# A transformer block with self- and cross-attention: GpSimd's part of the first stage moved and reordered, differences issued ahead of bases, and the first cross step's maxima ahead of the next query projection

## The reference

```python
def _attn(xq, ctx, wq, wkv, wo, bo):
    q = _heads(xq @ wq)
    k, v = jnp.split(ctx @ wkv, 2, axis=-1)
    q = _rope(q, sq, cq); k = _rope(k, sk, ck)
    a = jax.nn.softmax(jnp.einsum('bhnd,bhmd->bhnm', q, k) * DH ** (-0.5), axis=-1)
    return jnp.einsum('bhnm,bhmd->bhnd', a, v) ... @ wo + bo
def _adaln(x, c, lw, lb, gw, gb, bw, bb):
    return _ln(x, lw, lb) * (1.0 + (c @ gw + gb)) + (c @ bw + bb)
x = _attn(_adaln(x, ...), _adaln(x, ...), ...) + x
x = _attn(_adaln(x, ...), _ln(context, ...), ...) + x
x = gelu(_adaln(x, ...) @ ff_w1 + ff_b1) @ ff_w2 + ff_b2 + x
```

## Time and profile before

| what | value |
| --- | --- |
| median of 3 runs | 2149.64 us (2148.78 to 2154.3) |
| profiled execution, its own time | 2151.02 us |
| its span | 2149.2 us |
| TensorE busy | 2040.5 us, 95% |
| VectorE busy | 1751.1 us, 81% |
| ScalarE busy | 1429.1 us, 66% |
| GpSimd busy | 18.1 us, 1% |
| mean granted TensorE clock | 0.981 of full speed |

### The profile page before, as it was taken

How to read it: one execution, slowest core, us unless ns; L and a number is a source line. 1 busy time by engine, 2 the same in 40 slices (tenths; PEclk the granted TensorE clock), 3 DMA queues, 4 the chain that set the end, 5 groups by cost and what they waited for, 6 DMA issues and landing times. The chain is left out here.

```text
span 2149.2 us, 43063 instructions
## 1 busy us (share of the span) xinstructions
PE 2040.5 (95%) x17544; PEld 934.3 (43%) x17544; DVE 1751.1 (81%) x2720; ACT 1429.1 (66%) x1844; POOL 18.1 (1%) x16
## 2 busy tenths in 40 slices
PE   4799999999999999999999999999988999979999
PEld 2233333345333334533333453333633455446676
DVE  6899899986999998699989779987588888754754
ACT  4588778774787777577787657786457666652452
POOL 3000000000000000000000000000000000000000
PEclk8899999999999999999999999999998999999999
DMA  6010111011111111111011012021332344333111
GB/s 204 30 40 31 60 40 41 31 60 41 61 41 40 51 41 41 41 60 60 31 41 41 31 51 80 31 56 35 102 113 91 106 145 141 105 101 109 40 40 40
DMA packets 100347, 136.62 MB, mean 64 GB/s; under 512 B 34533, under 2 KB 73399, under 8 KB 100151
## 3 DMA queue, kind: packets, MB, share of 16 engines
q1 hardware_dynamic: 100151, 133.88, 18.9%
HBM read 68.34 MB, written 13.11 MB: 38 GB/s over the span
## 5 line engine op out<-in xcount | busy, mean ns | idle before, releaser
L713 ACT ACTIVATE sa_probs<-sa_ps_s 128x1024 f32<-128x1024 f32 x512 | 496.1, 1022 | 130.9 <-PE sa_ps_s L490 130.8
L505 PE MATMUL sa_ps_o<-sa_probs,sa_v_pair 128*64 128x512 f32 x2048 | 531.0, 609 | 1.4 <-DVE sa_mx L895 1.4
L908 DVE TENSOR_TENSOR sa_acc<-sa_acc,sa_probs 128x1024 f32<-128x1024 f32 x384 | 452.7, 1220 | 19.8 <-ACT sa_probs L713 11.9
L895 DVE CUSTOM_DVE_ANT_0 sa_rise<-sa_ps_t,sa_rise 128x512 f32<-128x512 f32 x504 | 327.3, 687 | 121.8 <-PE sa_ps_t L467 121.6
L483 PE MATMUL sa_ps_s<-scores_or_weights 64*128 64x512 f16 x3072 | 374.8, 376 | 1.5 <-ACT raw_or_keys L687 1.5
L701 ACT ACTIVATE sa_rise<-sa_ps_t 128x1024 f32<-128x1024 f32 x252 | 257.4, 1021 | 140.8 <-PE sa_ps_t L460 139.4
L483 PEld LDWEIGHTS sa_ps_s<-scores_or_weights 64*128 64x128 f16 x3072 | 151.9, 94 | 156.1 <-ACT sa_v_pair L692 6.8
L505 PEld LDWEIGHTS sa_ps_o<-sa_probs,sa_v_pair 128*64 128x64 f32 x2048 | 115.8, 135 | 149.8 <-issue 126.8
L460 PE MATMUL sa_ps_t<-sa_kd,scores_or_weights 64*128 64x512 f16 x504 | 99.3, 389 | 19.3 <-ACT scores_or_weights L697 6.8
L460 PEld LDWEIGHTS sa_ps_t<-sa_kd,scores_or_weights 64*128 64x128 f16 x504 | 25.2, 93 | 201.1 <-issue 163.1
L467 PE MATMUL sa_ps_t<-scores_or_weights 64*128 64x512 f16 x504 | 98.1, 385 | 11.3 <-ACT sa_rise L701 11.2
(11 more groups left out here) (338 smaller groups left out, 3656.2 us busy)
## 6 DMA issues: line engine op xcount, KB each, us to landing
sa_swp<-raw_or_keys SPq DMA_DIRECT2D x124, 256.0 KB, 2.4
sa_inv<-sa_scratch SPq DMA_DIRECT2D x128, 128.0 KB, 2.9
ca_swp<-raw_or_keys SPq DMA_DIRECT2D x64, 256.0 KB, 2.4
ca_inv<-ca_scratch SPq DMA_DIRECT2D x64, 256.0 KB, 3.9
sa_xs<-in_x SPq DMA_DIRECT2D x4, 1024.0 KB, 5.7
sa_xr<-in_x SPq DMA_DIRECT2D x4, 1024.0 KB, 6.8
x_after_cross<-scores_or_weights SPq DMA_DIRECT2D x32, 128.0 KB, 2.2
ff_xr<-x_after_cross SPq DMA_DIRECT2D x4, 1024.0 KB, 6.3
```

The lines of the kernel that those rows point to most:

```text
L505: ins = pe.matmul(ps_o[rows(x), half(c)], v_pair[:, kt, rows(x)], probs[:, kt % 2, c, half(x)], start=(kt == 0), stop=(kt == NK - 1))
L713: act.activation(probs[:, kt % 2, c, :], ps_s[c][:, :], ACT.Exp, scale=float(DH) ** -0.5).then_inc(s_p, 1)
L895: dve.tensor_tensor_reduce(out=larger, in0=max_banks(j, t)[:, half(x)], in1=larger, scale=1.0, scalar=-3.0e38, op0=ALU.add, op1=ALU.max, a ...
L908: dve.tensor_tensor(acc[:, c, :], before, probs[:, kt % 2, c, :], ALU.add).then_inc(s_acc[c], 1)
```

## The change

In self-attention four things are moved. GpSimd now also casts the two halves of the key weights (ScalarE did), as its first work. Its two subtractions for key and query of pair 0 go behind its work on the context, and it waits for the first bases before that. VectorE's weights_low of the key weights stand between the first affines. TensorE issues differences(0, t + 1) ahead of bases(0, t).

In cross-attention bases(0) goes ahead of the projection of query 2 on TensorE, all context values come ahead of both, the gate matmuls go behind project(3), and on VectorE maxima(0) goes ahead of turned(1), while tables() goes to the beginning of step 1. No instruction is added or removed; two casts change their engine.

```diff
--- before.py
+++ after.py
@@ -418,13 +418,14 @@
 
         @block.gpsimd
         def _(pool):
+            for n in range(2):
+                pool.wait_ge(s_w[n // 2], 32)
+                pool.tensor_scalar(weights[n][1], staged[:, n, :], WS, None, ALU.mult).then_inc(s_whi, 1)
             for n in range(4):
                 pool.wait_ge(s_nhi, n + 1)
                 pool.tensor_tensor(norm_out(xT_lo, 0, n), xn_first[:, n, :], norm_out(xT_hi, 0, n),
                                    ALU.subtract).then_inc(s_nlo, 1)
-            for i in range(2):
-                pool.wait_ge(s_hi[i], 1)
-                pool.tensor_tensor(lo[:, 0, i, :], raw[:, i, :], hi[:, 0, i, :], ALU.subtract).then_inc(s_lo[i], 1)
+            pool.wait_ge(s_base, 1)
             pool.wait_ge(s_cst, 7)
             for b in range(B):
                 ins = pool.tensor_scalar(cs[:, b, :], cs[:, b, :], c_mv[:, b, 0:1], c_rstd[:, b:b + 1],
@@ -433,6 +434,9 @@
             for i, op in enumerate((ALU.mult, ALU.add)):
                 pool.wait_ge(s_cn, i + 1)
                 pool.tensor_tensor(cs[:], cs[:], crow[:, i:i + 1, :].broadcast_to([M, B, DC]), op).then_inc(s_cn, 1)
+            for i in range(2):
+                pool.wait_ge(s_hi[i], 1)
+                pool.tensor_tensor(lo[:, 0, i, :], raw[:, i, :], hi[:, 0, i, :], ALU.subtract).then_inc(s_lo[i], 1)
 
         @block.tensor
         def _(pe):
@@ -571,10 +575,10 @@
             pe.wait_ge(s_kq_r[1], 2)
             differences(0, 1)
             for t in range(TT):
-                bases(0, t)
                 if 1 <= t < TT - 1:
                     maxima_free(0, t - 1, 2)
                     differences(0, t + 1)
+                bases(0, t)
                 if t == TT - 2:
                     pe.wait_ge(s_kq_r[0], 4)
                     context_transposes()
@@ -777,7 +781,8 @@
                 normalise(0, q)
             for n in range(4):
                 norm_high(0, n)
-            for n in range(4):
+            act.wait_ge(s_whi, 2)
+            for n in range(2, 4):
                 weights_high(n)
             for i in range(2):
                 for c in range(2):
@@ -1048,7 +1053,9 @@
             tables()
             for n in range(4):
                 first_affine(n)
-            for n in range(4):
+                if n < 2:
+                    weights_low(n)
+            for n in range(2, 4):
                 weights_low(n)
             context_variances()
             dve.wait_ge(s_rope, 32)
@@ -1433,6 +1440,15 @@
                                        xs[:, 4 * (n % 2) + q, n // 2 * P:(n // 2 + 1) * P], ident[:, :])
                 ins.then_inc(s_ntr, 1)
 
+            def gate_products():
+                pe.wait_ge(s_par, 16 * 8)
+                for i in range(2):
+                    for m in range(KD):
+                        for k in range(KD):
+                            ins = pe.matmul(ps_gate[:, i, m, :], gates[:, i, k, m * P:(m + 1) * P], condT[:, k, :],
+                                            start=(k == 0), stop=(k == KD - 1))
+                ins.then_inc(s_gate, 1)
+
             def ff_transposes(n):
                 pe.wait_ge(s_nxc, 2 * TT)
                 for q in range(4):
@@ -1507,31 +1523,29 @@
 
             for pair in range(PAIRS):
                 context_keys(pair)
-            for j in range(3):
+            for j in range(2):
                 for c in range(2):
                     if j >= 1:
                         pe.wait_ge(s_q_r, 2 * (j - 1) + c + 1)
                     project(j, c)
-                if j == 1:
-                    for n in range(2 * B):
-                        context_values(n)
+            for n in range(2 * B):
+                context_values(n)
             pe.wait_ge(s_init, 6)
             pe.wait_ge(s_bo, 32)
             pe.wait_ge(s_cev, 4 * PAIRS // 2)
-            pe.wait_ge(s_par, 16 * 8)
-            for i in range(2):
-                for m in range(KD):
-                    for k in range(KD):
-                        ins = pe.matmul(ps_gate[:, i, m, :], gates[:, i, k, m * P:(m + 1) * P], condT[:, k, :],
-                                        start=(k == 0), stop=(k == KD - 1))
-            ins.then_inc(s_gate, 1)
+            pe.wait_ge(s_low, 1)
+            pe.wait_ge(s_hi, 1)
+            bases(0)
+            for c in range(2):
+                pe.wait_ge(s_q_r, 2 + c + 1)
+                project(2, c)
             pe.wait_ge(s_low, 2)
             for g in range(G):
                 pe.wait_ge(s_hi, g + 1)
                 if g >= 1:
                     pe.wait_ge(s_p, 2 * g)
-                bases(g)
                 if g >= 1:
+                    bases(g)
                     values(g - 1)
                 pe.wait_ge(s_max, g + 1)
                 pe.wait_ge(s_q_r, 2 * min(g + 3, G))
@@ -1567,6 +1581,8 @@
                     if g >= 1:
                         pe.wait_ge(s_sum_r, g)
                     project(g + 3, 1)
+                if g == 0:
+                    gate_products()
                 if g in FF_TRANSPOSE:
                     pe.wait_ge(s_mt_r, g + 1)
                     ff_transposes(2 * FF_TRANSPOSE.index(g))
@@ -1899,10 +1915,14 @@
             low_keys(0)
             turned(0)
             low_keys(1)
+            maxima(0)
             turned(1)
             low(0)
             for g in range(G):
-                maxima(g)
+                if g == 1:
+                    tables()
+                if g >= 1:
+                    maxima(g)
                 if g + 1 < G:
                     low(g + 1)
                 if g >= 3:
@@ -1917,8 +1937,6 @@
                     turned(g + 2)
                 if g in STATS:
                     variances(g)
-                if g == 0:
-                    tables()
                 if g in FF_STATS:
                     ff_variances(g)
                 for u, tiles in enumerate((STATS, FF_STATS)):
```

## The result

The changed kernel takes 2158.24 us (median of 8 runs, 2155.08 to 2161.08) against 2150.26 us (8 runs of before beside them, 2147.28 to 2154.3). The ratio is 1.0034 with an interval of 1.0021 to 1.0047: slower by 0.34%. That is 8.0 us between the medians and 7.3 us (4.5 to 10.1) by the ratio, where 9.0 was forecast. The profiled span is 2154.7 us against 2149.2.

The account below looks back on a forecast made before the run. TensorE, busy 95% of the span, was taken as the bound. Start 1.65, stall and order of differences together 5.75 and cross-attention 1.6 summed to 9.0 us, so 2158.6 us against a median of 2149.64; range 4.4 to 15 us slower.

Parts of the forecast that it names:

- The bound and where to look: TensorE, busy 95%, paces the kernel; delays in the first 75 us of self-attention and 20 us of cross-attention delay everything.
- The stall: Self-attention, pair 0: ScalarE's copy waits for GpSimd's key subtraction behind 7.75 us of context work; relu 2 comes 5.4 later.
- rival (c): Self-attention: not slower, as GpSimd finishes before ScalarE's copy needs it; sum +1.6 us, chance 0.07.
- The round: Maxima loop of pair 0: maxima, differences and bases in series take 2.36 us a round instead of 2.16.
- The start, GpSimd scaling the key weights: Start of self-attention: GpSimd's scalings hold VectorE's small instructions, so TensorE starts at 25.85 instead of 24.21, +1.65 us.
- D: Duration of one GpSimd scaling of a 128x1024 key-weight tile at the start: taken as 2.06 us, bounds 1.0 and 5.3.
- Rival (a): Start: GpSimd is quick at a one-input operation, D 1.0 to 1.5; sum 6.9 to 8.0 us, chance 0.22.
- rival (b): Start: scaling costs per element like the 192-element row, D 3 to 5.3; sum 11 to 15.5 us, chance 0.12.
- Cross-attention: First 20 us of cross-attention: TensorE waits for query 2's copy, gates delay bases(1) by 2.3, 0.81 returns later; +1.6 us.
- Rival (d): Cross-attention gains as its waits of 2.78 and 1.54 us close: -2.4 there, sum 5.0 us, chance 0.15.
- The sum: Whole kernel: 9.0 us slower, a median of 2158.6 us.
- line delay: Cross-attention: the DMA of the line of maxima lies behind a 2 x 256 KB transfer; 0.4 us added, from 0 to 1.3.

Follow-up runs that it names:

- late-subtractions kernel: Kernel before with only GpSimd's two subtractions moved behind the context work, which waits for the first bases: 2157.13 us, ratio 1.0032.
- subtractions-first kernel: Changed kernel, but GpSimd, after waiting for the first bases, makes its two subtractions ahead of the context work: 2150.21 us, ratio 1.0002 to before.
- casts alone: Kernel before with only the two key-weight casts on GpSimd and their weights_low between the affines: 2151.90 us, ratio 1.0003.
- quiet kernel: Kernel before with GpSimd's subtractions after VectorE's last rotation and some weight casts, low parts and context roots moved into ScalarE and VectorE gaps: 2147.53 us, ratio 0.9994.
- early parameters: Kernel before with the eight parameter DMAs of cross-attention's gates issued ahead of the first query's swap: 2149.45 us, ratio 0.9993.

## Why the prediction was right

**The bound and where to look.** Right. TensorE is busy for 95% before and after, no busy time grew on it, and a delay of 7.3 us at the end of pair 0's maxima, with what cross-attention added, came out as 8.0 us of time.

**The stall.** Right in its mechanism and, step by step, in its sizes. With the 0.97 of the start added to each forecast: relu 0 at 44.01 (forecast 44.01), GpSimd let go at 45.70 (45.70), the copy at 55.72 (55.52), relu 2 at 56.22 (56.07), maxima(2) at 57.94 (57.77). Part of this closeness is luck. From the first projection to relu 0 it took 20.75 us in the profile of before and 18.83 in that of the change, the 1.92 forecast; but four other kernels with the subtractions in their old place took 19.69 to 20.23, and the two others with them behind the first bases took 18.00 and 18.05. The first projections' matmuls, in pairs, got faster (from 0.67 to 0.40 us a pair) at 29.7 us in the profile of before and at 30.7 in that of the change, but between 27.0 and 28.4 in these six.

The late-subtractions kernel shows that this part alone is enough, the subtractions-first kernel that without it nothing is left. So rival (c), not slower, falls at the place that the prediction named: the decision was whether GpSimd's 9.8 us of work fits in front of the copy.

**The round.** Mis-sized by 0.09: 2.45 instead of 2.36. Bases to maxima takes 0.68 where I took 0.64, and from the start of maxima to the next differences it is 1.37 where I had 1.32 (and twice 0.61 and 0.08 make 1.30). Over the rounds behind the stall and the last one, that makes maxima(7) 0.4 later, and 0.17 stood already at maxima(2), so stall and order are 7.29 − 0.97 = 6.3 instead of 5.75. The order alone costs 1.9 us in a row of eight rounds without a stall. Behind the stall it costs 0.75: from relu 0 to maxima(7) it is 25.47 us with both (69.48 − 44.01) and 24.72 in the late-subtractions kernel.

**The start, GpSimd scaling the key weights.** This is the term that was wrong in its working: +1.65 forecast, +0.97 in the profile of the change and +0.3 in that of the casts alone. Its steps failed in opposite directions and nearly cancelled. D is 2.77, not 2.06; with it the forecast's own chain would have given over +3. But the step that follows, that tables() is held until the second scaling ends and the first affine starts at 17.7, is false: it started at 15.15. The rows fit a hold of VectorE's instructions with two SBUF tensors for the first 0.9 to 1.0 us of each cast only (below). What followed took longer instead, 10.03 us from the first affine to TensorE's start (25.18 − 15.15) and not 8.15: the first weights_low had to wait for the first cast, which ended at 16.4, and the two of them took 2.05 and 2.17 us beside GpSimd where the chain had 1.15 each. The DMA, too, let GpSimd begin at 13.63 and not at 13.1. Rival (a), a quick cast, and rival (b), one that costs per element like the 192-element row, both lose their condition by D = 2.77, between (a)'s 1.5 and (b)'s 3. The time could not have told this, 8.0 us is also the upper end of (a)'s sum; the rows do.

**Cross-attention.** +1.6 forecast. The mechanism was right: TensorE waits for the copy of query 2 (4.75 us), and the gates (1.95 us) stand in front of bases(1). Counted from the end of ScalarE's copies of values, the copy of query 2 ended 2.0 later than before, where 1.85 was forecast. At bases(1) the kernel with this part alone shows +1.5, where +2.3 was forecast; at step 3 it shows +0.6 to +1.3, by which kernel it is held against, and nothing at step 9; its time can't be told from none. Two sizes were off: the line of maxima, issued 0.64 behind the second swap, held nothing up, as the shift matmuls follow its issue by 1.98 us (2.31 before), where I had added 0.4; and I let nothing be given back behind step 2, where the rest of the 1.5 us was gone by step 9. Also, 2.3 less 0.81 is 1.5, and I wrote 1.6. Rival (d), a gain of 2.4, did not show: the waits of 2.78 and 1.54 us were replaced by one of 4.75.

**The sum.** From the rows: 0.97 + 6.3 + 0.6 = 7.9 us, against 8.0 between the medians. That they meet so closely is luck: the start was 0.3 in another kernel, cross-attention is anything from 0 to 1.3, and the ratio's interval reaches from 4.5 to 10.1 us. The lower end of my range also doesn't follow from its reasons: D = 1, no line delay and 1.5 for the clock make 5.0, not 4.4. The span of the one profiled execution grew by 5.5 only. Between the end of the maxima and cross-attention the changed kernel lost another 2.85 us in that execution (10.15 − 7.30). The same stretch, from the first multiply after the maxima to cross-attention, took 1475.6 to 1479.3 us in the ten profiles of this study, in code that is the same in all of them. The changed kernel's is the longest of the ten, but the kernels that differ from before only behind this stretch already lie between 1475.6 and 1478.5, so a difference of 2.85 can't be taken for an effect of the change. From there to the end it took 604.66 us against 609.31 before, which gives 4.65 back; the ten profiles have 604.0 to 609.7, and the kernel with the casts alone, coded there as before, 603.96. For the same reason the gain of the quiet kernel and of the early parameters can't be read from one profile.

## What to carry to other kernels

Before work is put in front of an engine's short duty, look for who waits for that duty through a buffer that is reused: here a 2 us subtraction of GpSimd held ScalarE's copy, and with ScalarE's queue TensorE and VectorE stood still, so 7.7 us of unhurried context work became 6 to 7 us of time. A quiet VectorE is worth having, but the release of the buffer comes first: with the two subtractions at the head of the list the late start of GpSimd's work cost nothing that could be measured. When one hole appears in three engines at once (here 7 to 10 us), look first at the engine whose releaser is not among the three: here that was ScalarE, released by GpSimd.

## What the runs showed of the hardware

**A one-input instruction on GpSimd held VectorE only at its beginning.** All VectorE instructions here read two SBUF tensors, and what one took beyond its usual time is counted as a wait ahead of it. The casts ran from 13.63 and 16.38 for 2.77 us each. The gam instruction, at 13.73, took 0.96, where the next of its kind took 0.15, and so was free at 14.54, 0.91 after the cast began. The two bet instructions behind it took 0.15 and 0.17, as without a cast, with 1.4 us of the cast still to run. The first weights_low, at 16.44, took 2.05 instead of 1.15 and was free at 17.34, 0.96 after the second cast began. In the kernel with the casts alone, with another offset, gam at 13.63 took 0.41, free 0.91 after the cast's start at 12.98, and in the kernel with the subtractions first, gam at 13.59 took 0.68, free 0.91 after the cast's start at 13.21. The two-input subtractions held VectorE to their end, as in the earlier trace rows (3.14 instead of 1.22). By the Trainium skill, SBUF — State Buffer, section "SBUF: two separate sides", the exclusion lasts for the whole instruction; the subtractions agree with it, the casts do not. Why the casts let go early was not tried.

**GpSimd's prices.** Cast of 128x1024 with a constant factor: 2.77 us. Subtraction of 128x1024: 2.06 to 2.1 us. Two-step tensor_scalar of 77x192: 1.0 us. The cast lies between the two bounds of the prediction (1.0 and 5.3). It differs from the 77x192 row in its operations, output type and partitions as well as its length, so how the price grows with length alone is not shown.

**How much a run varies.** Kernels whose code is the same up to relu 0 start it at 43.8 to 45.0 us, and single runs of a kernel lie up to 11 us apart. Differences of 0.03 to 0.07% could not be told from none in five rounds, and one of 0.10% only just (1.0001 to 1.0018).
